# Two weight steps on 128 columns at a time, and two waits put before the gathers of tiles 1 and 2

## The reference

```python
emb = embed_table[f_ix, x_idx]                              # 2048 x 26 x 16
lin1 = w1_table[f_ix, x_idx].sum(axis=1, keepdims=True) + w1_bias
s = emb.sum(axis=1)
fm = 0.5 * ((s * s).sum(-1) - (emb * emb).sum(axis=(1, 2)))[:, None]
h = relu(emb.reshape(n, 416) @ mlp_w1 + mlp_b1)
h = relu(h @ mlp_w2 + mlp_b2)
mlp_out = h @ mlp_w3 + mlp_b3
x0 = emb.transpose(0, 2, 1); last = x0; feats = []
for W in (cin_w0, cin_w1, cin_w2):                          # K = 128
    last = einsum('ndl,ndf,klf->ndk', last, x0, W)
    feats.append(last)
cin = concatenate(feats, axis=-1).sum(axis=1) @ lin_w + lin_b
out = lin1 + fm + mlp_out + cin
```

## Time and profile before

| what | us |
|---|---|
| median of 3 runs | 507.5 (507.06 to 509.96) |
| span of the profiled execution | 805.6 |
| busy PE, PEld, DVE, ACT, POOL in it | 502.1, 407.8, 406.0, 387.1, 356.7 |

### The profile page before, as it was taken

How to read it: one execution, slowest core, us unless ns; L and a number is a source line. 1 busy time by engine, 2 the same in 40 slices (tenths; PEclk the granted TensorE clock), 3 DMA queues, 4 the chain that set the end, 5 groups by cost and what they waited for, 6 DMA issues and landing times.

```text
span 805.6 us, 6956 instructions
## 1 busy us (share of the span) xinstructions
PE 502.1 (62%) x2307; PEld 407.8 (51%) x2307; DVE 406.0 (50%) x668; ACT 387.1 (48%) x759; POOL 356.7 (44%) x369
## 2 busy tenths in 40 slices
PE   3100039869394865839295766839295766849997
PEld 3100037648273654628274555638274645638766
DVE  6000014478183644728183654738183645738776
ACT  0000022887172644727272644627172744628876
POOL 6777700287527172644527172635527171630000
PEclk9999999989688886979688896959688896969999
DMA  8622202641102020111102020111102020110000
GB/s 180 105 8 7 7 11 22 164 130 7 6 3 7 2 7 3 6 4 6 6 3 7 2 7 4 6 5 4 6 2 9 1 8 2 6 4 2 0 1 1
DMA packets 21492, 15.49 MB, mean 19 GB/s; under 512 B 12837, under 2 KB 19794, under 8 KB 21330
## 3 DMA queue, kind: packets, MB, share of 16 engines
q0 software_dynamic: 11648, 3.19, 11.8%
q1 hardware_dynamic: 6805, 9.86, 5.0%
q10 hardware_dynamic: 3005, 2.01, 1.2%
HBM read 14.83 MB, written 0.21 MB: 19 GB/s over the span
## 4 chain that ended last, share of the span: by engine, by line
another core or an unknown queue 37%; PE 26%; ACT 17%; DVE 13%; issue 6%; DMA 1%; ACTq 0%; DVEq 0%
ACT ps_s L582 5%; ACT z_hi L575 5%; DVE z_lo L787 4%; PE ps_s L1081 2%; PE ps_q L1095 2%; PE ps_q L1096 2%; PE ps_q L1097 2%; PE ps_y L1181 2%; ACT room_a L581 2%; PE ps_s L1069 2%; PE ps_y L1182 2%; PE ps_q L1019 1%; ACT by_pos L552 1%; ACT z_hi L577 1%
## 5 line engine op out<-in xcount | busy, mean ns | idle before, releaser
L484 POOL DMA_INDIRECT emb<-rows,idx_raw x364 | 356.3, 979 | 357.4 <-ACT first_all L533 247.9
L575 ACT ACTIVATE z_hi<-ps_s 128x512 fp32r<-128x512 f32 (+1 forms) x192 | 114.2, 595 | 256.9 <-remote 196.0
L787 DVE TENSOR_TENSOR z_lo<-ps_s,z_hi 128x512 fp32r<-128x512 f32 (+1 forms) x192 | 132.0, 688 | 172.0 <-ACT ps_s L582 152.7
L1181 PE MATMUL ps_y<-look_hi,one_hot 128*128 128x442 f32 x208 | 85.2, 410 | 115.8 <-DVE emb L932 61.4
L582 ACT ACTIVATE ps_s<-ps_s 128x512 f32<-128x512 f32 (+1 forms) x192 | 113.7, 592 | 0.7
L1181 PEld LDWEIGHTS ps_y<-look_hi,one_hot 128*128 128x128 f32 x208 | 45.4, 219 | 123.8 <-DVE emb L932 67.7
L1095 PE MATMUL ps_q<-z_lo,zw_hi 128*127 128x512 f32 (+1 forms) x192 | 87.5, 456 | 21.0 <-issue 11.5
L928 DVE SCALAR_TENSOR_TENSOR ps_y<-tables,look_place,ps_y 128x442 f32<-128x442 f32 x52 | 35.1, 675 | 98.2 <-remote 98.2
L1182 PE MATMUL ps_y<-look_lo,one_hot 128*128 128x442 f32 x208 | 82.6, 398 | 0.0
L1096 PE MATMUL ps_q<-z_hi,zw_lo 128*127 128x512 f32 (+1 forms) x192 | 79.7, 415 | 0.0
L1097 PE MATMUL ps_q<-z_hi,zw_hi 128*127 128x512 f32 (+1 forms) x192 | 79.7, 415 | 0.0
(11 more groups left out here) (190 smaller groups left out, 892.0 us busy)
## 6 DMA issues: line engine op xcount, KB each, us to landing
emb<-rows,idx_raw POOLq DMA_INDIRECT x364
w_space<-rows SPq DMA_DIRECT2D x2, 728.9 KB
m_space<-rows SPq DMA_DIRECT2D x2, 728.9 KB
w_space<-key_scratch SPq DMA_DIRECT2D x1, 1408.0 KB
w<-cin_w SPq DMA_DIRECT2D x2, 416.0 KB, 4.8
w<-cin_w ACTq DMA_DIRECT2D x2, 416.0 KB, 7.6
w_space<-cin_w SPq DMA_DIRECT2D x2, 416.0 KB
w_space<-cin_w ACTq DMA_DIRECT2D x2, 416.0 KB
```

The source lines that it names most:

```text
L484: pool.indirect_dma_start(emb[t % EMB][:, f, :], None, rows, bass.IndirectOffsetOnAxis(row_ix[:, t, f:f + 1], 0)).then_inc(gathered[t] if ...
L575: act.activation(z_hi[0:k, c, :], ps[0:k, :], ACT.Square)
L787: z = dve.tensor_tensor(z_lo[0:k, u % NC, :], ps, z_hi[0:k, u % NC, :].bitcast(F32), ALU.subtract)
L1181: pe.matmul(o, one_hot[n % 2][:, j, :], look_hi[i][:, ws], start=(j == 0), stop=False)
```

## The change

Steps 1 and 2 take each field in one call on all 128 columns, 26 calls a step instead of 52, and so wait for both halves of their weights before the first call. In POOL's stream, tile 1's gathers also wait for s_blocks (the last folded product), and tile 2's for zw_hi_ready at 4 (the main weights' high part).

```diff
@@ gpsimd
             for t in range(T):
                 if t < 2:
                     pool.wait_ge(ix_ready, t + 1)
+                if t == 1:
+                    pool.wait_ge(s_blocks, 1)
+                if t == 2:
+                    pool.wait_ge(zw_hi_ready, 4)
                 if t >= EMB:
@@ tensor
             pe.wait_ge(lin_in, 16 * 3)
             for h in range(2):
-                ls = slice(HALF_P * h, HALF_P * (h + 1))
                 pe.wait_ge(w2_in[h], 16 * 2)
-                for g in range(F):
-                    mm = pe.matmul(ps_y[ls, g:g + 1], w2[:, ls, g], lin[:, 2:3], start=True, stop=True)
+            for g in range(F):
+                mm = pe.matmul(ps_y[:, g:g + 1], w2[:, :, g], lin[:, 2:3], start=True, stop=True)
             mm.then_inc(m_done, 1)
 
             pe.wait_ge(m_copied, 2)
             for h in range(2):
-                ls = slice(HALF_P * h, HALF_P * (h + 1))
                 pe.wait_ge(w1_in[h], 16 * 2)
-                for f in range(F):
-                    c = (f % HALF) * (F + 1)
-                    mm = pe.matmul(ps_q[f // HALF][ls, c:c + F + 1], w1[:, ls, f], m_lin2[:], start=True, stop=True)
+            for f in range(F):
+                c = (f % HALF) * (F + 1)
+                mm = pe.matmul(ps_q[f // HALF][:, c:c + F + 1], w1[:, :, f], m_lin2[:], start=True, stop=True)
             mm.then_inc(b_done, 1)
```

## The result

| | us |
|---|---|
| before, median (4 runs beside the change) | 508.7 |
| after, median of 4 runs | 520.5 (519.8 to 523.2) |
| ratio | 1.021 (95% interval 1.019 to 1.024) |

The change makes the kernel 2.1% slower, about 11 us. The profile of the kernel after has no stops of TensorE at all. Its span is 518.0 us and its own time 519.84, so 1.8 us lie around the span. The profile of before stands there with 805.6 us. A second profiled execution of the same kernel before (first experiment) spans 505.8 us, with a time of 507.64. It is the one to compare with, and it is called "the clean profile of before" from here on.

What follows compares the result with a forecast made beforehand. The prediction took POOL's row of gathers to bound the kernel: 507.5 us measured before plus 11.4 us that POOL loses waiting at tile 1 gives 518.9, so 519 us. The range was 504 to 522 us.

Steps and rivals of the forecast that it cites:

- POOL's row is the bound: Whole kernel: POOL's 364 gathers, 463.0 us without waits, set the time, so early stops are paid at the end.
- The stops belong to the profile and not to the time: Step 1 and loop: TensorE's stops, 287.4 us of waits in the profile, can't be in the timed runs in full.
- Theory B: Setup and loop: TensorE's stops are partly real in timed runs, holding gathers back frees the setup; 497.5 us, chance 0.12.
- One sign that I gave: Profile after, weight step 1: it should still stop while tile 0's gathers run, but no longer for 91 us.
- 7.4 us around the span and the landing: End of kernel: from the summed 500.1 to 507.5 us, tile 14's last gather landing plus time around the span.
- A pass costs 0.22, so no gain from half the calls: Weight steps 1 and 2: a strided 128-column pass takes 0.22 us, so 52 passes take 11.4 us a step.
- a strided pass costs 0.11: Rival, weight steps: 128 strided columns take 0.11 us; 513.1 us if POOL bounds, 504.8 if the engines do; chance 0.18.
- w1's second half decides step 2 at 25.5: Start of weight step 2: it waits for w1's second half, taken at 25.5 us, and ends 3.1 us later than before.
- POOL loses 11.4 us: Tile 1's first gather on POOL: it starts at 48.0 instead of 36.6 us, held by the last folded product.
- Nothing else is lost: Sum for the whole kernel: POOL's 11.4 us is the only loss added to 507.5 us.
- Tiles 1 and 2 are hidden: by_pos copies of tiles 1 and 2: their gathers arrive before the copies need them, tile 2 by 1 us or so.
- the engines are the bound: Rival, whole kernel: POOL has slack and hides the wait, only 3.1 us of later setup count; 510.6 us, chance 0.25.

Runs made afterwards that it cites:

- first experiment: The kernel before, unedited, profiled a second time; ratio 1.000 (0.998 to 1.002), profiled span 505.8 us.
- the dose of the two signals: The changed kernel with tile 1's gathers waiting instead for the end of weight step 2 (ratio 1.002) or for the summed rows, by_row_done (1.040).
- the cut gathers: 20 instead of 22 gathers in each of tiles 3 to 15: on the kernel before 0.9935 (503.4 us), on the changed kernel 1.0146 (513.9 us).
- e14_pieces_warm: The kernel before with DVE's long subtractions in four pieces and warm-up matmuls on TensorE ending as step 1 begins; ratio 0.9925, 503.8 us.

## Why the prediction was right, step by step

- **POOL's row is the bound.** Right, by the clean profile, the dose of the two signals and the cut gathers. It is the bound by little: 4 us before the engines take over.
- **The stops belong to the profile and not to the time.** Right. Theory B's 497.5 never came near. One sign that I gave did not come: step 1 no longer stops at all in the profile after.
- **7.4 us around the span and the landing.** Mis-sized: 1.8 us lie around the span and 2.2 between the gather's end and the copy that needs it. The rest was an error in the sum for POOL's row, which put the 342nd gather's end at 438.8; in the clean profile it ends at 443.3. From the copy to the end are 60.3 us instead of 61.3. Since I added the change to the measured 507.5, this didn't reach the forecast.
- **Step 1 starts at 12.** It started at 13.7.
- **A pass costs 0.22, so no gain from half the calls.** The number was right (0.228), the reason only half of it. I compared step 1 with contiguous rows from later in the kernel and read the factor of two as the stride. The stride does cost that factor at the high level (e14_pieces_warm). But steps 1 and 2 ran at the low level, and there contiguous weights cost 0.216 too. The rows that I compared stood at the high level, and the printed 1.00 of the early windows told nothing. That the number came out is partly luck: the two limits are nearly equal. The rival "a strided pass costs 0.11" was wrong as well: per column the price is the same for 64 and 128 columns.
- **w1's second half decides step 2 at 25.5.** Partly. In the profile after, step 1's end decided (25.6), and step 2 started at 25.9. In the seven other profiles of the 26 calls w1 did decide: step 2 waited 1.3 to 3.6 us for it and started between 26.2 and 28.2. The last folded product came 2.6 us later than before, I had 3.1; in those seven it came 3.2 to 5.0 us later.
- **POOL loses 11.4 us.** Mis-sized: 8.6. I let tile 1's first gather start at 36.6, read from the profile that had stopped. There DVE's m1_lo came after tile 0's gathers; in the clean profile it meets two of them, and tile 1 starts at 39.8. In the profile without tile 2's wait, which is the same work, POOL lost 11.0 us, as the signal came 2.4 us later.
- **Nothing else is lost.** Wrong by 3.7 us, the longer gathers. So 8.6 + 3.7 = 12.3 where I had 11.4: two errors that nearly cancel. That is luck, and both terms vary from one execution to the next.
- **Tiles 1 and 2 are hidden.** Wrong. Their copies waited 4.9 and 2.4 us. I gave the gathers their best pace (32.6 us a tile; 35.7 and 35.6 measured, with long gathers in both) and no time to land. The waits didn't change the sum, but they are why fewer gathers would not have hidden the change, where my rival "the engines are the bound" gave 510.6: with POOL relieved the loss stayed at 10.5 us.
- **Tile 2's wait costs nothing.** Right.
- **The moves of the blocks lose nothing beside gathers.** Right. From the end of the last folded product to the last zw_hi are 14.9 us in the clean profile and 14.5 with the calls alone, both with gathers running, and 14.5 in the profile after, where tile 1's had just been let go.

## What to carry to other kernels

Before a wait is put in front of work on a queue, ask what that queue is at the end of the kernel: if it is the one that never rests, each us that it stands idle early is paid late, and a reserve further on doesn't help the tiles next in line. A profile whose span is far from the time describes another execution. Take a second one before changing a kernel for what the first shows. Half as many calls of double width gain nothing where the price goes by the column. When two limits are about equal, an experiment that lifts one of them shows no gain and doesn't clear it: contiguous weights at the low clock, and the high clock with strided weights, each left the pace where it was.

## What the runs showed of the hardware

- In one profiled execution TensorE stood still for 287 us in total, in stretches that began while gathers ran; thirteen other profiles of the program and its variants show none. The cause is open.
- TensorE can be busy without a gap for 11 us and stay at 1.2 GHz: calls with 1 or 27 moving columns, in both steps, even behind a stretch at 2.4 GHz.
- fp32 weights with neighbouring columns 26 elements apart cost 1.8 ns a column and pass at the high and at the low level; contiguous ones cost 0.84 at the high level and 1.7 at the low one.
- A clock printed as 1.00 ahead of the first clock record says nothing: the same matmuls were 0.43 us apart before that record and 0.23 after it.
- A gather that meets one of DVE's long subtractions of two fp32 SBUF tensors takes 1.6 to 2.8 us instead of 0.94 (clean profile); with the subtractions in four pieces 1.2 to 1.9, and once 2.6.
